# Overflow experts' weights: a copy by ScalarE from the resident pairs in place of a second fetch from HBM

## The reference

```python
x = x + attention(xn) + ffn(xn)
# attention: decayed linear attention in 16 heads, layernorm, times silu(xn @ wg.T), projected by wo
# ffn, on the 1024 tokens xf, 32 experts of 192 hidden features, the best 4 for each token:
logits = xf @ router_w.T + router_b
top_vals, top_idx = top_k(logits, 4)
rw = softmax(top_vals) * 1.8
g = silu(einsum('th,eih->tei', xf, gate_w)); u = einsum('th,eih->tei', xf, up_w)
routed = einsum('tei,ehi,te->th', g * u, down_w, combine)     # combine holds rw at the chosen experts
shared = (silu(xf @ shared_gate_w.T) * (xf @ shared_up_w.T)) @ shared_down_w.T
ffn = routed + shared
```

## Time and profile before

| | us |
|---|---|
| three runs | 289.6, 287.49, 293.31 (median 289.6) |
| the profiled execution | 287.65 |
| its span, from first to last instruction | 285.8 |
| mean granted TensorE clock in it | 0.903 |
| busy in the span: PE, DVE, POOL, ACT | 218.1, 137.3, 128.1, 62.9 |

### The profile page before, as it was taken

The page is one execution under the profiler, slowest core; times in us unless marked ns, Lnnn a source line. Parts: engine busy times, 40 slices in busy tenths (PEclk is TensorE's granted clock), DMA queues, the critical chain, the costliest instruction groups (busy, mean ns, idle before and its releaser), DMA issues.

```text
span 285.8 us, 4514 instructions
## 1 busy us (share of the span) xinstructions
PE 218.1 (76%) x1586; PEld 154.4 (54%) x1586; DVE 137.3 (48%) x415; ACT 62.9 (22%) x177; POOL 128.1 (45%) x156
## 2 busy tenths in 40 slices
PE   7599879788399989795999685996895999980000
PEld 2477546555266656554887574665672867830000
DVE  2943989998727582825251403140331234330394
ACT  2131321111001111120231313130322133310240
POOL 2044060425707064644157473737374654443471
PEclk9999999999689999996899997999599699997555
DMA  6989999100000002010104899979949981113972
GB/s 178 405 266 349 349 348 350 60 2 1 0 3 1 2 0 57 0 55 0 39 18 119 286 348 354 354 241 326 338 143 274 309 267 61 42 56 91 358 256 92
DMA packets 41335, 48.59 MB, mean 170 GB/s; under 512 B 2837, under 2 KB 38106, under 8 KB 41184
## 3 DMA queue, kind: packets, MB, share of 16 engines
q1 hardware_dynamic: 37424, 38.87, 42.1%
q0 software_dynamic: 3456, 8.92, 9.6%
q10 hardware_dynamic: 432, 0.50, 0.7%
HBM read 41.99 MB, written 6.82 MB: 171 GB/s over the span
## 4 chain that ended last, share of the span: by engine, by line
PE 53%; DVE 16%; POOL 10%; DMA 6%; another core or an unknown queue 5%; issue 5%; ACT 2%; SPq 1%; POOLq 0%; DVEq 0%
PE bank L1269 15%; PE bank L1281 4%; PE bank L1110 4%; DMA w_early<-y_rows 3%; PE bank L1285 3%; PE bank L1126 3%; PE bank L1141 3%; PE bank L1237 3%; PE bank L1249 3%; POOL arena L607 3%; DVE x_sb L1034 2%; PE bank L1294 2%; PE bank L1203 2%; POOL arena L618 2%
## 5 line engine op out<-in xcount | busy, mean ns | idle before, releaser
L635 POOL DMA_INDIRECT y_rows<-y_mem,codes x36 | 36.2, 1007 | 41.3 <-DVE y_mem L940 32.2
L607 POOL TENSOR_SCALAR arena<-arena,cst 128x256 f32<-128x256 f32 x16 | 14.6, 924 | 64.8 <-ACT arena L487 56.6
L932 DVE TENSOR_TENSOR h_mem<-h_mem,bank 128x128 f32<-128x128 f32 x32 | 9.2, 287 | 64.8 <-issue 24.0
L627 POOL DMA_INDIRECT xg_mem<-xn_rows,codes x36 | 35.3, 981 | 10.4 <-issue 9.8
L1269 PE MATMUL bank<-xb_mem,w_early 128*128 128x128 f32 x216 | 29.7, 288 | 9.8 <-DVE h_mem L934 4.5
L1269 PEld LDWEIGHTS bank<-xb_mem,w_early 128*128 128x128 f32 x216 | 27.5, 202 | 10.5 <-issue 6.2
L882 DVE TENSOR_TENSOR arena<-bank,arena 128x512 f32<-128x512 f32 x32 | 20.5, 682 | 11.5 <-PE bank L1141 11.5
L1269 PE MATMUL bank<-xb_mem,arena 128*128 128x128 f32 x168 | 22.6, 294 | 0.2 <-issue 0.2
L1269 PEld LDWEIGHTS bank<-xb_mem,arena 128*128 128x128 f32 x168 | 21.7, 210 | 0.9 <-issue 0.9
L940 DVE COPY y_mem<-bank 128x256 f32<-128x256 f32 x36 | 13.8, 419 | 15.6 <-remote 7.9
L1141 PE MATMUL bank<-arena 32*128 32x256 f32 x128 | 18.1, 400 | 3.2 <-DVE arena L882 3.2
(11 more groups left out here) (156 smaller groups left out, 369.9 us busy)
## 6 DMA issues: line engine op xcount, KB each, us to landing
w_early<-w_exp_dram SPq DMA_DIRECT2D x9, 1152.0 KB, 12.8
w_early<-w_ovf_dram SPq DMA_DIRECT2D x16, 512.0 KB
arena<-w_exp_dram SPq DMA_DIRECT2D x7, 1152.0 KB
w_early<-y_rows SPq DMA_DIRECT2D x8, 512.0 KB, 8.0
x_sb<-x_dram SPq DMA_DIRECT2D x4, 256.0 KB, 5.7
arena<-w_qkvg_dram SPq DMA_DIRECT2D x2, 512.0 KB, 7.7
arena<-decay_dram SPq DMA_DIRECT2D x1, 1024.0 KB, 10.2
xn_rows<-arena SPq DMA_DIRECT2D x2, 512.0 KB, 3.2
```

The costliest lines, as they stand in the source:

```text
L607: nc.gpsimd.tensor_scalar(qeo[:, t % 2, par * KT * P:(par + 1) * KT * P], q, cst[:, C_PM + par:C_PM + par + 1], None, ALU.mult).then_inc(q ...
L627: nc.gpsimd.indirect_dma_start(xg[:, k % RING, :], None, xn_rows, bass.IndirectOffsetOnAxis(ap=codes[:, c, 0:1], axis=0),).then_inc(tok_in ...
L635: nc.gpsimd.indirect_dma_start(y_rows, bass.IndirectOffsetOnAxis(ap=codes[:, c, 1:2], axis=0), ysb[:, k % YRING, :], None, bounds_check=RO ...
```

## The change

The weights of all 16 pairs get places of their own in one tensor, `w_mem`, and stay there. A pair's layout becomes two equal parts: each expert has its 1024 columns of gate, up and down (`XW`), and then 128 columns with half of the pair's shared last part. The memory behind pair 15 (`o_mem`) holds one overflow group. ScalarE fills it: for each sub-block it reads the expert's number into a register and copies 1024 columns from the place in `w_mem` that the number selects. SyncE fetches only the 64 KB of `w_ovf2` for each sub-block. Since the place is one for all groups, both wait for the down products of the group before (`od_ps`). The 512 KB fetches are gone. Pair p of 9 to 15 is issued one step earlier. The groups start in steps 8, 10, 12 and 14, and the order of results is told apart from that of gathers (`SEQ_Y`). In a step the hidden transposes now stand ahead of gate and up of unit 2s, and the down products of the group behind them. Since gate and up now have the same columns as in a pair, their SiLU and their product are two instructions each.

```diff
-O_BASE = (5, 8, 11, 14)
-O_HOME = (0, 3 * PW, 6 * PW, 0)
-O_FREES = (2, 5, 8, None)
+O_BASE = (8, 10, 12, 14)
...
-        w_early = sb("w_early", [P, EARLY * PW])
-        arena = sb("arena", [P, 21650])
+        w_mem = sb("w_mem", [P, EARLY * PW + 21650])
+        w_early = w_mem[:, 0:EARLY * PW]
+        arena = w_mem[:, EARLY * PW:EARLY * PW + 21650]
+        o_mem = w_mem[:, PAIRS * PW:PAIRS * PW + SUBS * OW]
...
-            def overflow_in(first, home, signal):
+            def overflow_in(first, signal):
 
                 for j in range(SUBS):
                     e = sp.value_load(eid_row[0:1, bass.ds(first + j, 1)], min_val=0, max_val=E - 1)
-                    o = home + j * OW
-                    sp.dma_start(w_early[:, o:o + OW - D].rearrange("p (c d) -> p c d", d=D),
-                                 w_ovf[bass.ds(e * OPIECES, OPIECES)].rearrange("c p d -> p c d")).then_inc(signal, 16)
-                    sp.dma_start(w_early[0:I2, o + OW - D:o + OW], w_ovf2[bass.ds(e * I2, I2), :]).then_inc(signal, 16)
+                    sp.dma_start(o_mem[I2:P, j * OW + XW:(j + 1) * OW], w_ovf2[bass.ds(e * I2, I2), :]).then_inc(signal, 16)
...
             def paced_pair(p):
-                sp.wait_ge(dn_ps, 2 * (p - EARLY + 1))
+                need(sp, dn_ps, 2 * (p - EARLY))
                 pair_in(p)
 
-            for p in range(EARLY, 12):
+            for p in range(EARLY, PAIRS):
                 paced_pair(p)
...
+            for j in range(STATIC_O):
+                need(sp, od_ps, j)
+                overflow_in(SUBS * j, wo_in[j])
...
+            def copy_weights(i, j):
+
+                e = act.value_load(eid_row[0:1, bass.ds(i, 1)], min_val=0, max_val=E - 1)
+                return nc.scalar.copy(o_mem[:, j * OW:j * OW + XW], w_mem[:, bass.ds(e * EW, XW)])
+
+            def copy_static(b, j):
+                need(act, od_ps, b)
+                copy_weights(SUBS * b + j, j).then_inc(ow_sb, 1)
 
             def expert_step(s):
                 if s + 1 < PAIRS:
                     take_pair_tokens(s + 1)
-                if s in O_BASE:
-                    take_overflow_tokens(O_BASE.index(s))
-                if 0 < s < PAIRS:
-                    gate_unit(2 * s)
+                if s - 1 in O_BASE:
+                    copy_static(O_BASE.index(s - 1), 1)
                 if s - 2 in O_BASE:
                     act.wait_ge(oht_ps, O_BASE.index(s - 2) + 1)
                     take_overflow_hidden().then_inc(oht_sb, 1)
+                if 0 < s < PAIRS:
+                    gate_unit(2 * s)
+                if s in O_BASE:
+                    take_overflow_tokens(O_BASE.index(s))
+                if s - 1 in O_BASE:
+                    copy_static(O_BASE.index(s - 1), 2)
+                    copy_static(O_BASE.index(s - 1), 3)
                 if s < PAIRS:
                     gate_unit(2 * s + 1)
+                if s in O_BASE:
+                    if s == O_BASE[0]:
+                        act.wait_ge(eid_sb, 1)
+                        for p in range(PAIRS):
+                            act.wait_ge(we_in[p], 16)
+                    copy_static(O_BASE.index(s), 0)
                 if s - 1 in O_BASE:
                     act.wait_ge(og_ps, O_BASE.index(s - 1) + 1)
-                    gate_overflow().then_inc(osil_sb, 1)
+                    gate_overflow(osil_sb)
...
                     if j >= 1:
-                        pe.wait_ge(ys_sb, AT["O", j - 1] + 1)
-                    pe.wait_ge(wo_in[j], 16 * 2 * SUBS)
-                    overflow_gate_up(O_HOME[j]).then_inc(og_ps, 1)
+                        pe.wait_ge(ys_sb, Y_AT["O", j - 1] + 1)
+                    pe.wait_ge(ow_sb, SUBS * (j + 1))
+                    pe.wait_ge(wo_in[j], 16 * SUBS)
+                    overflow_gate_up().then_inc(og_ps, 1)
```

More of the change, by code:

```diff
@@ L32 @@
 MB = 3 * P
-EW = KT * MB + D
+XW = KT * MB + D
+EW = XW + P
 PAIRS = E // 2
-PW = 2 * EW + D
+PW = 2 * EW
+EARLY = 9
 PIECES = PW // D
-OPIECES = 4
-EARLY = 9
 SUB = 32
 SUBS = P // SUB
-OW = KT * 2 * I + 2 * D
+OW = XW + D
 STATIC_O = 4
@@ L121, in token_blocks, with result_order, build @@
     return seq
+def result_order():
+    seq = []
+    for s in range(1, PAIRS + 1):
+        pair, o = [("P", 2 * s - 2), ("P", 2 * s - 1)], [("O", O_BASE.index(s - 2))] if s - 2 in O_BASE else []
+        seq += o + pair if s < PAIRS else pair + o
+    return seq
 SEQ_X = token_blocks()
 AT = {b: k for k, b in enumerate(SEQ_X)}
-COLUMN = [n if kind == "P" else E + n for kind, n in SEQ_X]
+SEQ_Y = result_order()
+Y_AT = {b: k for k, b in enumerate(SEQ_Y)}
+SENT = [sum(k % YRING == w for k in range(len(SEQ_Y))) for w in range(YRING)]
 X_ORDER = [b for b in SEQ_X if b[0] == "O" or b[1] % 2 == 0]
 X_AT = {b: k for k, b in enumerate(X_ORDER)}
-def build(nc, x, consts, decay, w_router, w_qkvg, w_out, w_sgu, w_sd1, w_sd2, lnwb, rbias, w_exp, w_ovf, w_ovf2, xn_rows, y_rows, out):
+def build(nc, x, consts, decay, w_router, w_qkvg, w_out, w_sgu, w_sd1, w_sd2, lnwb, rbias, w_exp, w_ovf2, xn_rows, y_rows, out):
     with ExitStack() as ctx:
@@ L618, in gate_output, with column @@
                 nc.gpsimd.tensor_tensor(z[:, t % 2, :], z1[:, :], gate[:, t % 3, :], ALU.mult).then_inc(z_sb, 1)
+            def column(b):
+                return b[1] if b[0] == "P" else E + b[1]
             def gather(k):
@@ L625, in gather @@
                 pool.sem_inc(pool_go, 1)
-                c = COLUMN[k]
+                c = column(SEQ_X[k])
                 nc.gpsimd.indirect_dma_start(
@@ L633, in scatter @@
                 pool.sem_inc(pool_go, 1)
-                c = COLUMN[k]
+                c = column(SEQ_Y[k])
                 nc.gpsimd.indirect_dma_start(
@@ L955, in expert_step @@
                     middle()
+                if s - 2 in O_BASE and s < PAIRS:
+                    overflow_result(O_BASE.index(s - 2))
                 if s < PAIRS:
@@ L1292, in overflow_gate_up @@
                         rows = slice(SUB * j, SUB * (j + 1))
-                        o = home + j * OW + g * 2 * I
-                        last = nc.tensor.matmul(ps_og[rows, 0:2 * I], xbO[:, g * P + SUB * j:g * P + SUB * (j + 1)],
-                                                w_early[:, o:o + 2 * I], start=(g == 0), stop=(g == KT - 1),
+                        o = j * OW + g * MB
+                        last = nc.tensor.matmul(ps_og[rows, 0:MB], xbO[:, g * P + SUB * j:g * P + SUB * (j + 1)],
+                                                o_mem[:, o:o + MB], start=(g == 0), stop=(g == KT - 1),
                                                 skip_group_check=True)
@@ L1436, in expert_weights @@
                 wg, wu = feature_major(gate, e, g), feature_major(up, e, g)
-                pairs += [wg[:, :P], wu[:, :P]] + ([wu[:, P:], wg[:, P:]] if j == 0 else [wg[:, P:], wu[:, P:]])
+                pairs += [wg[:, :P], wu[:, :P], wu[:, P:], wg[:, P:]]
             pairs.append(down[e, :, :P].T)
-        pairs.append(np.concatenate([down[2 * p, :, P:].T, down[2 * p + 1, :, P:].T], axis=0))
+            pairs.append(np.concatenate([down[2 * p + i, j * P:(j + 1) * P, P:].T for i in range(2)], axis=0))
     w_exp = np.concatenate(pairs, axis=1).reshape(P, PAIRS * PIECES, D).transpose(1, 0, 2)
     w_exp = np.ascontiguousarray(w_exp)
-    w_ovf = np.concatenate([gate.transpose(0, 2, 1)[:, :P], up.transpose(0, 2, 1)[:, :P],
-                            gate.transpose(0, 2, 1)[:, P:], up.transpose(0, 2, 1)[:, P:],
-                            down.transpose(0, 2, 1)[:, I2:]], axis=2)
-    w_ovf = w_ovf.reshape(E, P, OPIECES, D).transpose(0, 2, 1, 3)
-    w_ovf = np.ascontiguousarray(w_ovf).reshape(E * OPIECES, P, D)
-    w_ovf2 = np.ascontiguousarray(down.transpose(0, 2, 1)[:, :I2]).reshape(E * I2, D)
-    return w_exp, w_ovf, w_ovf2
+    w_ovf2 = np.ascontiguousarray(down.transpose(0, 2, 1)[:, P:]).reshape(E * I2, D)
+    return w_exp, w_ovf2
 def kernel(**inp):
```

128 lines of the change are left out of this document (59 added, 69 removed).

## The result

The changed kernel took 298.71 us (median of four runs, 295.98 to 306.6); the kernel before took 288.78 beside it (287.49 to 293.31). The ratio is 1.033, with a 95% interval from 1.020 to 1.046: slower, by 3% or so (the lower end lies just at the 2% that a measurement here can tell). Executions of one kernel on one chip fall into a faster and a slower group, and every ratio with an interval compares only the faster ones, while medians are of all. 281.0 had been forecast, with a range up to 291.

The account below looks back on a forecast made before the run. The prediction took TensorE's expert stage as the bound, with 24.5 us lost mostly beside SyncE's overflow fetches. 287.65 - 15.9 (fetches removed) + 8.3 (copies) = 280.1, put at 281 us with half the run's offset from the median; range 271 to 291.

Parts of the forecast that it names:

- the removed term: Expert stage: dropping the 16 overflow fetches of 512 KB was to save 15.9 us of TensorE's 24.5 us lost.
- 8.6: Expert stage: the us of TensorE's loss taken to stay, out of 24.5, once the 512 KB fetches are gone.
- Rival 3: Expert stage: gaps come from something else, say GpSimd's gathers and scatters, so only the copies count; 296.0 us; chance 0.1.
- The opening: Fourth to seventh slice, nine pairs under way: full DMA engines without the expert stage's gaps; evidence all 24.5 us might go.
- Rows 7: Profile rows of the fourth to seventh slice: DMA engines full, TensorE's longest idle time 2.09 us, for VectorE.
- rival 1: Expert stage: the gaps vanish entirely with the fetches, all 24.5 us saved; 271.5 us; chance 0.2.
- The copies: ScalarE's 16 copies of 128x1024: TensorE waits for them ahead of each group's gate/up, adding 8.3 us, from 6.3 to 15.5.
- 3c - 1.43: TensorE's wait ahead of a group's gate/up, c being the copy period; 2.17 us at c = 1.2.
- rival 2: ScalarE's copies: reading the expert's number isn't hidden, c = 1.7 us; 287.3 us, no difference; chance 0.18.
- TensorE never waits for one of these fetches to land: Expert stage of the kernel before: no TensorE wait was put down to pair or overflow fetches landing.
- The small fetches' wait: SyncE's four 64 KB fetches per group: 0.7 us late at the group's gate/up, covered by the copies' 2.17.
- The extra SiLU and product: Each group's added instructions, 0.27 us each, lie under down and the next transposes and cost nothing.

Follow-up runs that it names:

- g2c: Kernel before without any SyncE fetch in the expert stage, gathers and scatters kept, on a chip with late signals; 289.39 us, ratio 0.998.
- g1c: Kernel before without the 24 gathers in the expert stage, fetches and scatters kept, on a chip with late signals; 272.68 us, ratio 0.935.
- i1: Changed kernel without the 24 gathers in the expert stage; 271.37 us, ratio 0.983 to the kernel before.
- e4: Kernel before without its overflow fetches (16 of 512 KB and 16 of 64 KB), pairs 9 to 15 still fetched; 267.56 us.
- e2: Changed kernel with its 16 small fetches cut to an eighth of their bytes; 279.38 us, ratio 1.012 to the kernel before.
- b2: Kernel before, unaltered, profiled on the third set's chip, without late signals; 276.03 us.
- b1: Kernel before, unaltered, one more profile on the second set's chip, with late signals; 295.63 us.
- a1: Changed kernel, unaltered, run again on the second set's chip, with late signals; 303.68 us, ratio 1.044 to the kernel before.

## Why the prediction was wrong

**The step that failed** is the removed term: "By the place of the gaps, the 6.0 of the pairs stay and 18.4 go", and with it 15.9 us saved. The gaps were put beside SyncE's issues, since both lay in the same stretches. But before's DMA engines are busy from 157 to 236 us, save one slice: nearly any gap in the stage lies beside some fetch. GpSimd's rows were in the same trace, and late signals end just behind one (rows over at 158.8, 171.9 and 218.2 us, signals taken at 160.6, 173.4 and 219.3). With all fetches gone nothing is gained (g2c, ratio 0.998), with a third of GpSimd's operations gone 6.5% (g1c, ratio 0.935). In the profile of after 28.3 us are lost, not 8.6.

**Rival 3** named this cause and GpSimd by name, and gave 296.0; it got a chance of 0.1. Its "against" was weak. That the four overflow stretches held three quarters of the gaps (18.4 of 24.4 us) in that one profile came of something else, since g2c loses as much without any of those fetches. And GpSimd's scatters after 237 us come two or three at a time until TensorE is nearly done, since no gathers are left to stand between them. The Trainium skill, page "SBUF — State Buffer", section "Who interferes with whom", says that DMA never contends with a compute engine. For SyncE's fetches the runs agree on a chip with late signals (g2c, ratio 0.998); what the fetches cost on the other kind is a wait for them to land. Of signals late beside GpSimd's rows that section gives no warning.

**The opening as evidence.** Rows 7 were read as "full DMA engines alone don't do it", which g2c bears out from the other side: the gaps come without full engines too. That GpSimd issues no gathers in the opening was written down under rival 1 only.

**The copies** were right in mechanism and place, and a bit high in size. 8.3 us forecast; 7.6 measured clean (i1 against e4), with waits of 2.01, 1.65, 1.64 and 1.57, where 3c - 1.43 gives 1.57 at c = 1.0. The length was taken as 1.12 us and is 1.043. The page "VectorE: DVE Perf Modes" of the Trainium skill, section on the TRN2 errata, gives by its 224 + N cycles an estimate of 1.04 us, and the trace agrees with 1.043; so this figure was nearer than the one worked out from the rows. The 0.496 of the earlier trace rows is of another kind of operation, an activation that reads a factor from `rw` for each partition. Reading the number is hidden as taken, two copies in a row take 1.98 us; rival 2 falls. What was missed is that the copies stand behind late signals too: the waits are 2.64 and twice 2.92 us then, 10.05 us over the four groups.

**"TensorE never waits for one of these fetches to land"** was true of that one trace only. Where signals are on time, step 6 waits 6.2 us. So a gain that the change can bring exists (10.7 us of the stage on such a chip), though not the one that was forecast, and is given back there by the copies (7.6) and pair 15 (step 9 at 14.5 us against 8.5 in i1, 6.0). 87.5 - 10.7 + 7.6 + 6.0 = 90.4 for its stage; e2, the nearest to the changed kernel run on such a chip, has 91.1 and a ratio of 1.012 (0.994 to 1.030), which can't be told from no change. The changed kernel itself wasn't run on one.

**Moved work.** The small fetches' wait was hidden, as taken; three of the four waits of L1320 end with a copy, and the fourth, for which the profile has no clear end, is 1.57 us as in i1, where it ends with one. The extra SiLU and product don't show in any wait.

**The sum, term by term,** for the profiled execution: 287.65 + 7.6 (structure) + 4.3 (more lost to late signals) + 1.1 (step 3 starts later, 157.16 against 156.06) - 0.6 (behind TensorE's end) = 300.05. The sum was forecast as 287.65 - 15.9 + 8.3: the second term has the wrong sign, the third is right to within 1 us. That the time came near rival 3's 296.0 fits its mechanism, "only the copies count", but for the 4.3.

## What to carry to other kernels

When gaps and a transfer lie side by side, ask how many of the gaps would lie beside it by chance, and look for a second thing that is there in them: here most late signals ended just behind a row of GpSimd's DMAs. Such a coincidence is no proof either, as the stall itself can end the row; a run with all fetches away and one with the gathers away tell. Copies put ahead of other work on an in-order engine cost their own time once, and again whatever their start is held up by. And a time taken on one chip may hide a wait that decides on the next, so compare a run only with the kernel before on the same chip.

## What was not expected of the hardware

- The same kernel takes 288.8, 291.8 and 292.4 us (medians) in three sets of runs and 275.3, 278.9 and 277.1 in three others, each set on one chip. On the first kind TensorE's signals reach the other engines 3 to 6 us late in stretches, on the second none does, though GpSimd's rows are longer there (24 and 27 operations in b2). Why chips differ isn't known from these runs.
- On the first kind most late stretches (37 of 46) end 0.2 to 2.0 us behind the end of a row in which GpSimd issues gathers and scatters back to back. GpSimd's spans are rough, and that the gathers are the cause rests on the one kernel with them left out, on one chip (g1c). What in the chip holds the signal isn't known. In g2c a row of four that began 4.3 us behind the one before it (at 207.02) had no late signal with it.
- On the same chips TensorE also pauses where no other engine holds it by the profile: 3.7 us in all in the first profile of before, 11.1 in b1, 10.9 in g2c, but 0.2 in a1, and none in g1c or b2. So it may be more than signals that is held.
- A ScalarE copy of 128x1024 float32 from SBUF to SBUF takes 1043 ns and two in a row take 1.98 us, the register read before each one hidden.
